# Four graph layers on one core: in the last hop of the first layer, ScalarE's copy and square of an older batch go ahead of its copy of the present batch

## The reference

```python
edge_index = jnp.stack([src, dst])
A = 0.9 * segment_softmax(leaky_relu(s_h + s_t + s_r), head_ids)      # per edge, 4 heads
def step(Z, _):                                                        # 5 times
    msgs = A[:, :, None] * Z[tail_ids]
    return segment_sum(msgs, head_ids) + 0.1 * Z0, None
out = Z.reshape(N, 4 * 64) @ W_o                                       # 256 -> 64
x = layernorm(x + out)
```

## Time and profile before

| | us |
|---|---|
| median of 3 runs (lowest to highest) | 11049.81 (11042.33 to 11066.14) |
| the profiled execution, its own time | 11056.49 |
| span of its trace | 11054.7 |
| VectorE busy | 6769.6 (61% of the span) |
| GpSimd busy | 7208.5 (65%) |
| TensorE busy, matrix products | 5819.0 (53%) |
| ScalarE busy | 2887.5 (26%) |
| hop4, first chain input to last row product (4236 to 5103) | 867 |

### The profile page before, as it was taken

How to read it: one execution, slowest core, us unless ns; L and a number is a source line. 1 busy time by engine, 2 the same in 40 slices (tenths; PEclk the granted TensorE clock), 3 DMA queues, 4 the chain that set the end, 5 groups by cost and what they waited for, 6 DMA issues and landing times. The chain is left out here.

```text
span 11054.7 us, 113652 instructions
## 1 busy us (share of the span) xinstructions
PE 5819.0 (53%) x26903; PEld 4127.3 (37%) x26903; DVE 6769.6 (61%) x14006; ACT 2887.5 (26%) x5217; POOL 7208.5 (65%) x7087
## 2 busy tenths in 40 slices
PE   3757999100000004666777776767674558722255
PEld 2352333000000004665556565555553447622234
DVE  8953332595878785665767665878775766511127
ACT  0042222001222223333434443222221322100045
POOL 3755777587777776444767665767777767677720
PEclk9978999555555555666877777777776665555578
DMA  0073333163545453224766565655444999611158
GB/s 14 7 252 101 71 72 71 42 201 104 165 148 165 148 165 95 81 84 123 217 200 222 189 203 178 222 192 152 131 136 126 316 249 121 95 47 46 46 186 244
DMA packets 1454720, 1555.31 MB, mean 141 GB/s; under 512 B 1037506, under 2 KB 1158688, under 8 KB 1454491
## 3 DMA queue, kind: packets, MB, share of 16 engines
q1 hardware_dynamic: 1191816, 1284.78, 36.7%
q0 software_dynamic: 252160, 248.38, 12.3%
q10 hardware_dynamic: 10514, 19.71, 0.5%
HBM read 883.57 MB, written 800.52 MB: 152 GB/s over the span
## 5 line engine op out<-in xcount | busy, mean ns | idle before, releaser
L2601 POOL DMA_INDIRECT r_got<-state,comb_src x1176 | 1183.2, 1006 | 432.5 <-issue 344.3
L312 POOL DMA_INDIRECT payload_or_bias_rows<-payload,place x784 | 907.4, 1157 | 483.5 <-issue 254.3
L1446 POOL DMA_INDIRECT hop_got<-edges_b,next_col x784 | 808.6, 1031 | 537.4 <-ACT hop_got L1684 278.5
L1796 PE MATMUL hop_ps_into<-hop_out,span_s 128*128 128x256 f32 x8 | 4.9, 713 | 2050.4 <-DVE hop_out L1620 2050.4
L1446 POOL DMA_INDIRECT hop_got<-edges_a,next_col x784 | 782.3, 998 | 259.5 <-issue 238.4
L1796 PEld LDWEIGHTS hop_ps_into<-hop_out,span_s 128*128 128x128 f32 x8 | 2.0, 312 | 2052.7 <-DVE hop_out L1620 2052.7
L1684 ACT COPY hop_got<-hop_zeros 128x1792 f32<-128x1792 f32 x224 | 377.4, 1685 | 1206.1 <-DVE hop_ps_msg L1571 1099.9
L1620 DVE SCALAR_TENSOR_TENSOR hop_out<-hop_out,hop_runs_now,hop_ps_msg 128x256 f32<-128x256 f32 x1176 | 565.5, 481 | 50.9
L2881 PE MATMUL r_ps_v<-dense1g,r_gt 128*128 128x128 f32 x3136 | 586.6, 360 | 0.0
L2881 PEld LDWEIGHTS r_ps_v<-dense1g,r_gt 128*128 128x128 f32 x3136 | 532.3, 263 | 133.0 <-issue 133.0
L2701 DVE SCALAR_TENSOR_TENSOR r_acc<-r_acc,r_runs_now,r_got 128x64 f32<-128x64 f32 x1173 | 334.8, 285 | 272.7 <-DMA r_got<-state,comb_src 229.6
(11 more groups left out here) (816 smaller groups left out, 17998.6 us busy)
## 6 DMA issues: line engine op xcount, KB each, us to landing
edges_a<-hop_out SPq DMA_DIRECT2D x112, 896.0 KB
edges_b<-hop_out SPq DMA_DIRECT2D x112, 896.0 KB, 4.3
r_in<-state SPq DMA_DIRECT2D x168, 448.0 KB
hop_side<-x_dst SPq DMA_DIRECT2D x280, 224.0 KB, 4.2
own<-plain_y SPq DMA_DIRECT2D x56, 952.0 KB
x_and_sums<-c_y SPq DMA_DIRECT2D x56, 896.0 KB
bn_in<-x_and_sums SPq DMA_DIRECT2D x56, 896.0 KB
r1a_in<-own SPq DMA_DIRECT2D x84, 448.0 KB
```

Of the source, the lines that this page charges most:

```text
L312: nc.gpsimd.indirect_dma_start(out=t.raw[:, n, :], out_offset=None, in_=t.pay[k], in_offset=bass.IndirectOffsetOnAxis(t.place[:, k, n:n + ...
L1446: pool.indirect_dma_start(out=got[:, u, c, :], out_offset=None, in_=table, in_offset=at, bounds_check=EP - 1, oob_is_err=False).then_inc(g ...
L2601: pool.indirect_dma_start(out=got[:, n, c - b * CT, :], out_offset=None, in_=table, in_offset=bass.IndirectOffsetOnAxis(idx[:, at + c:at + ...
```

## The change

In ScalarE's program of `edge_pass`, for the last hop only, the block that copies and squares the product of two batches back (`ago(KEEP)`, with `KEEP` = 2) is moved up. It stood at the end of the turn, behind the copies of the present batch's turned sums and turned node rows; it now stands between the zeroing of the gather buffer and those copies. For that the loop over `ago(0)` is split in two. The instructions, their waits and their signals are the same, and so are the programs of all other engines and all other kinds of hop.

```diff
--- before.py
+++ after.py
@@ -1691,6 +1691,15 @@
                         wait(act, *msg_used(i, u))
                         nc.scalar.activation(msg[:, u % 2].rearrange("p c d -> p (c d)"), ps_lin[:, 0:CT * D],
                                              ACT.Relu).then_inc(msg_ready[u], 1)
+                if rows_too:
+                    for i, u in ago(KEEP):
+                        act.wait_ge(x_product[u], i + 1)
+                        past(act, v_kept, i, u, 2, 16)
+                        past(act, y1_ready, i, u, 2)
+                        nc.scalar.copy(v[:, u % 2].rearrange("p c d -> p (c d)"), ps_o[:, u % 2, 0:CT * D]).then_inc(v_ready[u], 1)
+                        past(act, summed, i, u, 2)
+                        nc.scalar.activation(sq[:, u % 2].rearrange("p c d -> p (c d)"), ps_o[:, u % 2, 0:CT * D], ACT.Square).then_inc(sq_ready[u], 1)
+                for i, u in ago(0):
                     if turned:
                         act.wait_ge(rt_done, order(i, u) + 1)
                         past(act, product, i, u, 1)
@@ -1703,14 +1712,6 @@
                         past(act, x_product, i, u, 2)
                         nc.scalar.copy(xt[:, u % 2, 0:3 * P], ps_x[:, 0:3 * P])
                         nc.scalar.copy(xt[0:D, u % 2, 3 * P:], ps_x[0:D, 3 * P:]).then_inc(xt_read, 1)
-                if rows_too:
-                    for i, u in ago(KEEP):
-                        act.wait_ge(x_product[u], i + 1)
-                        past(act, v_kept, i, u, 2, 16)
-                        past(act, y1_ready, i, u, 2)
-                        nc.scalar.copy(v[:, u % 2].rearrange("p c d -> p (c d)"), ps_o[:, u % 2, 0:CT * D]).then_inc(v_ready[u], 1)
-                        past(act, summed, i, u, 2)
-                        nc.scalar.activation(sq[:, u % 2].rearrange("p c d -> p (c d)"), ps_o[:, u % 2, 0:CT * D], ACT.Square).then_inc(sq_ready[u], 1)
             for u in range(RING):
                 if kind == "cheb1":
                     act.wait_ge(msg_kept[u], ROUNDS * 16)
```

## The result

The changed kernel takes 10760.14 us, the median of 4 runs (10751.91 to 10770.19), against 11046.18 for the kernel before: the ratio is 0.9737, with a 95% interval of 0.9725 to 0.9749. The forecast was 10768, its range 10748 to 10850. The span of the profiled execution is 10764.2 us against 11054.7, 290.5 less. It leaves out the first of the waits at L1548, 4.96 us. The whole last hop, from the first batch's multiply-add (L1579) to the end of the last row product, is 585.6 us (4227.85 to 4813.46) against 877.0 (4226.24 to 5103.24), 291.4 less.

What follows compares the result with a forecast made beforehand. VectorE's wait for ScalarE's square was taken to bound the last hop: 286.8 us won less 5 for TensorE gives 282, so 10774.5 profiled; with the median 6.7 lower, 10768 us, range 10748 to 10850.

Steps and rivals of the forecast that it cites:

- The wait at L1548 goes in 53 turns, 286.8 us at most: Last hop: VectorE's wait for ScalarE's square goes in 53 of 55 cases, 285.8 us, plus 1.0 at the hop's end.
- VectorE is next, at 10.28 us a turn: Last hop: with the stall gone, a turn falls from 15.73 us to VectorE's own work, 10.28 us.
- TensorE late by 0.1 us a turn, 5 us: VectorE's wait at the chain's end for TensorE's product: 0.1 us a turn, 5 us taken off the gain.
- The nearest row: TensorE in the hop's second turn, square not yet waited for: turning to product's end 8.8 us, under VectorE's 10.28.
- half-way case: TensorE partly at 1.2 GHz in the last hop: 10.9 to 11.4 us a turn, 10795 to 10821 us.
- rival (a): TensorE becomes the bound at 1.2 GHz, 12.6 us a turn, 10885 us; chance 0.15 with its half-way case.
- the mix: TensorE's share of work at 1.2 and 2.4 GHz: 12.6 or 7.1 us a turn, 10.89 busy if unchanged.
- GpSimd at no cost, 9.5 us a batch: Last hop: a batch's seven gathers take 9.5 us, under VectorE's 10.28, with four batches of buffers between: no cost.
- rival (b): GpSimd's gathers become the bound beside a busy VectorE: 11.1 us a turn, 10805, or 12.2, 10862; chance 0.09.
- The flags with 0.7 us to spare: ScalarE's run flags ready at about 6.0 us, VectorE's chain starting at about 6.7: 0.7 us to spare, the tightest margin.
- (c): Slower: the moved copy, waiting for a store, holds ScalarE, TensorE's product and VectorE; first extra us gives 11103; chance 0.02.
- (d): VectorE's wait only changes its name, the turn stays 15.7 us, 11050 us; chance 0.02.

Runs made afterwards that it cites:

- The two halves: Against the kernel before, only the square moved ahead of the turned copies, 10818.7 us, or only the copy of the product, 11026.6 us.
- the dose: Against the kernel before, copy and square moved between the copies of the turned sums and those of the node rows: 11026.1 us.

## Why the prediction was right

- *The wait at L1548 goes in 53 turns, 286.8 us at most.* Right: all 291.8 us of it are gone. The two halves and the dose show that the stall was exactly what stood on ScalarE's path to the square: 24.0 us for the copy's 0.43 a turn, 27.8 for 0.52. Over the whole hop VectorE's idle time fell by 287.0 us (340.5 to 53.5), but that this is the prediction's 286.8 is in part luck. At the hop's end its waits went from 10.96 us to 6.6, 4.4 won and not 1.0, and a wait of 1.5 for a product near the start went too. Against that stand 3.9 us more of waits for gathers in the first turns and 1.0 for the run flags, at the table load, both of which the prediction put at nothing.
- *VectorE is next, at 10.28 us a turn.* Right, 10.22 in the mean: its own overlap of two instructions that follow each other without a wait (0.08 us at the turn's start) was not in the sum, 4.4 us over the hop. That and the 5 us of the next point are the 9.4 by which the gain of 282 was too small for the whole hop, 291.4.
- *TensorE late by 0.1 us a turn, 5 us.* Too careful: it stands 1.78 us a turn in the window, and VectorE never waits at the tail but for the last product. The nearest row, the hop's second turn at 8.8 us, was the right one to go by; the mean busy time per turn is now 8.4. The product is at 3.34 us in all 43 turns of the window. With the copy left behind (square only) it is 5.08 in the mean and TensorE is the bound, the half-way case of rival (a) at 11.3 us a turn. The prediction had the two states of the clock and took "the mix" as it was; it had no reason for the good one, and it put no price on the copy's part, which is 57 us of the hop (611.9 against 554.5). So that TensorE stayed clear of VectorE was in part luck. The reason is open still: the product is fast with no gap ahead of it in the changed kernel, slow with no gap in the kernel with 12 more clearings, and, in four turns, fast behind gaps longer than the mean in the square-only kernel.
- *GpSimd at no cost, 9.5 us a batch.* Right in result; its gathers grew from 1056 to 1110 ns in the same stretch, 9.9 us a batch, 0.3 under VectorE's turn, and it hardly waits for a buffer any more (0.6 us). The contention of rival (b) was real and small: in the kernel before, between 4300 and 4780, none of the 95 gathers that lay for the most part beside a standing VectorE took over 1.1 us, and 34 of the other 125 did.
- *The flags with 0.7 us to spare.* 0.78 in the turn shown, 0.59 to 1.36 in the window, and 1.01 us too late in the one turn with the table load.
- *Rivals (c) and (d)* show nowhere: L1699 waits for nothing, and no wait took the place of the one that went.
- *The total.* The profiled execution came out 8.5 us below the forecast (10766.0 against 10774.5): 9.4 in the hop, 0.9 back in the rest of the kernel. That the rest agrees so well is luck, given how far it differs between traces.

## What to carry to other kernels

When an engine's program serves several batches in a turn, put the work whose inputs are oldest ahead of the wait that ends last. The price of the wrong order can be read from one turn of the timeline: it is the idle time of the engine that waits, as long as the engine in between has a longer idle time of its own. A freed buffer can count twice: here the square let VectorE go on, and the copy ended a wait of TensorE, with which its product took 5.08 us in the mean in place of 3.34. And once the stall is gone, look for the next two bounds together; here VectorE's turn and GpSimd's gathers lay 0.3 us apart.

## What the runs showed of the hardware

TensorE, busy 440.00 of 440 us, was granted 0.65 with 12 more clearings per batch, and 1.00 with 24 more wide transposes in place of them (busy 404.37 of 440), which made the longer program no slower than the shorter one (10756.0 and 10760.1 us, with hops of 556.0 and 554.5). GpSimd's gathers took 1110 ns in the mean beside a VectorE that was busy 93% of the window, against 1056 beside one that was busy 61%. The same turning of 14 transposes took 1.75 us at a granted clock of 1.00 and up to 3.25 at 0.83. A VectorE copy of 0.13 us put between a reciprocal and the product that needs it cost nothing, since that product starts 0.22 us behind the reciprocal without it. And the rest of the kernel, outside the hop, differed from 10181.4 to 10236.2 us between 14 traces, so that a gain of 13 us inside the hop was seen in the median on one chip and not on another.
